# Scatter of the edge counts of a graph network: pieces of 127 sorted keys in place of 128

## The reference

```python
h = relu(layernorm(x))                                   # before each of the four
x = x + L0(h):  m = h[src] + edge_attr_96
                aggr = segment_sum(m, dst, 6250);  relu(aggr @ W1 + b1) @ W2 + b2 + (1 + eps) * h
x = x + L1(h):  msg = relu(h[src] + edge_attr_32 @ We + be)
                aggr = segment_sum(msg, dst, 6250);  two products, batch norm, relu
x = x + L2(h):  three graph convolutions: segment_sum(dinv[row] * dinv[col] * hw[row], col, 6250)
x = x + L3(h):  three attention layers: softmax over the edges of each target, weighted sum of h[src]
```

## Time and profile before

| what | us |
|---|---|
| median of the 2 runs | 12576.79 |
| the 2 runs | 12553.91 and 12599.67 |
| span of the profiled execution, first to last instruction | 12571.5 |
| GpSimd busy in it | 7982.0 (63%) |
| TensorE busy | 6178.3 (49%) |
| VectorE busy | 5097.4 (41%) |
| ScalarE busy | 4054.9 (32%) |

### The profile page before, as it was taken

The page is one execution under the profiler, slowest core; times in us unless marked ns, Lnnn a source line. Parts: engine busy times, 40 slices in busy tenths (PEclk is TensorE's granted clock), DMA queues, the critical chain, the costliest instruction groups (busy, mean ns, idle before and its releaser), DMA issues.

```text
span 12571.5 us, 140237 instructions
## 1 busy us (share of the span) xinstructions
PE 6178.3 (49%) x36085; PEld 5371.9 (43%) x36085; DVE 5097.4 (41%) x15838; ACT 4054.9 (32%) x10426; POOL 7982.0 (63%) x8396
## 2 busy tenths in 40 slices
PE   0199731255555567999344444433444334443443
PEld 0188621234444445777333333333334333343333
DVE  8455400033222224222444444444444444444444
ACT  0199400034444440000333333333333323333332
POOL 1877777557777750000677777667777766777775
PEclk8555665666666667999555555555555555555555
DMA  8044421222222214666222222222222222222222
GB/s 278 17 103 104 126 83 39 56 44 53 53 53 53 53 38 131 210 209 217 63 68 68 67 68 68 56 66 68 67 68 68 67 54 67 68 68 68 67 68 59
DMA packets 1053014, 1038.73 MB, mean 83 GB/s; under 512 B 641834, under 2 KB 758358, under 8 KB 1052336
## 3 DMA queue, kind: packets, MB, share of 16 engines
q1 hardware_dynamic: 704544, 611.05, 16.6%
q0 software_dynamic: 264160, 337.47, 13.2%
q10 hardware_dynamic: 83664, 82.78, 2.0%
HBM read 935.74 MB, written 96.55 MB: 82 GB/s over the span
## 4 chain that ended last, share of the span: by engine, by line
POOL 60%; issue 21%; PE 11%; DVE 4%; ACTq 2%; DMA 1%; ACT 0%; DVEq 0%; POOLq 0%; SPq 0%; PEldq 0%
POOL sb_HG L565 47%; POOL edge_counts L626 13%; PE sums L975 3%; ACTq L651 2%; PE psA L975 1%; PE psB L975 1%; PE sums L912 1%; PE psD L975 1%; PE psC L975 1%; PE psA L860 1%; DVE sb_ACC L1942 0%; PE psD L894 0%; PE psD L870 0%; PE psC L870 0%; PE psB L886 0%
## 5 line engine op out<-in xcount | busy, mean ns | idle before, releaser
L565 POOL DMA_INDIRECT sb_HG<-attention_table,sb_NOW x4992 | 4731.8, 948 | 1574.4 <-issue 1516.5
L912 PE MATMUL sums<-sb_HG 128*128 128x100 f32 x9984 | 2068.6, 399 | 443.9 <-ACT sb_HG L695 426.6
L912 PEld LDWEIGHTS sums<-sb_HG 128*128 128x128 f32 x9984 | 2035.4, 313 | 453.9 <-ACT sb_HG L695 435.6
L626 POOL DMA_INDIRECT edge_counts<-sb_HG x1625 | 1632.3, 1005 | 764.8 <-issue 495.0
L691 ACT ACTIVATE sb_H<-sb_iota_row,sb_H 128x128 f32<-128x128 f32 x6656 | 2029.1, 388 | 137.7 <-PE sums L912 63.9
L565 POOL DMA_INDIRECT sb_HG<-feature_table,sb_NOW x1612 | 1522.0, 944 | 556.3 <-issue 490.8
L1942 DVE TENSOR_TENSOR sb_ACC<-sb_ACC,sums 128x100 f32 x4992 | 1274.1, 255 | 1152.5 <-PE sums L912 619.0
L922 PEld LDWEIGHTS sums<-sb_HG 128*128 128x128 f32 x6656 | 1324.8, 299 | 315.4 <-issue 315.4
L922 PE MATMUL sums<-sb_HG 128*128 x6656 | 1340.6, 384 | 144.0 <-ACT sb_HG L695 71.3
L760 ACT ACTIVATE psC<-sb_SB 128x128 f32<-128x128 f32 x156 | 43.8, 281 | 3935.1 <-DVE sb_SB L1895 3935.1
L1487 DVE TENSOR_TENSOR sb_ACC<-sb_ACC,sums 128x97 f32 (+1 forms) x3328 | 848.0, 255 | 605.1 <-PE sums L922 135.9
(11 more groups left out here) (442 smaller groups left out, 9019.0 us busy)
## 6 DMA issues: line engine op xcount, KB each, us to landing
sb_HG<-edge_counts SPq DMA_DIRECT2D x1152, 256.0 KB, 3.3
sb_H<-rel_rows SPq DMA_DIRECT2D x312, 512.0 KB
sb_HG<-attention_table,sb_NOW POOLq DMA_INDIRECT x4992
sb_HG<-in_edge_attr_dram SPq DMA_DIRECT2D x201, 384.0 KB, 3.5
edge_counts<-sb_LW ACTq DMA_DIRECT2D x12, 6272.0 KB, 42.5
edge_counts<-sb_HG POOLq DMA_INDIRECT x1625
sb_HG<-feature_table,sb_NOW POOLq DMA_INDIRECT x1612, 2.5
sb_EA<-in_edge_attr_dram SPq DMA_DIRECT2D x201, 128.0 KB, 2.5
```

What stands on the lines that cost most here:

```text
L565: pool.indirect_dma_start(to, None, rows, bass.IndirectOffsetOnAxis(ap=index, axis=0)).then_inc(landed, 16)
L626: pool.indirect_dma_start(every_count, bass.IndirectOffsetOnAxis(ap=slot_of[:, f:f + 1], axis=0), tally[:, f:f + 1], None).then_inc(scatte ...
L912: last = nc.tensor.matmul(bank[:, k // 4, k % 4 * width:(k % 4 + 1) * width], HOT[:, hot, k, :], G[:, slot, k, 0:width], start=True, stop= ...
```

## The change

```diff
     CHUNKS = SORTED // P
+    CHUNK = P - 1
+    assert CHUNK * CHUNKS >= EF
...
-                    for f in range(p, SORTED, P):
-                        pool.indirect_dma_start(every_count, bass.IndirectOffsetOnAxis(ap=slot_of[:, f:f + 1], axis=0),
-                                                tally[:, f:f + 1], None).then_inc(scattered[n % 2], 16)
+                    for c in range(CHUNKS):
+                        f = P * c + p
+                        pool.indirect_dma_start(every_count, bass.IndirectOffsetOnAxis(ap=slot_of[0:CHUNK, f:f + 1], axis=0),
+                                                tally[0:CHUNK, f:f + 1], None).then_inc(scattered[n % 2], 16)
...
-                part, to = slice(c * P, (c + 1) * P), slice(c % 4 * P, (c % 4 + 1) * P)
-                nc.tensor.transpose(sums[c // 8][:, c // 4 % 2, to], low[:, part], ident[:, :])
-                nc.tensor.transpose((psA, psB, psC, psD)[c // 4][:, to], place[:, part], ident[:, :])
+                part, to = slice(c * CHUNK, (c + 1) * CHUNK), slice(c % 4 * P, (c % 4 + 1) * P)
+                nc.tensor.transpose(sums[c // 8][0:CHUNK, c // 4 % 2, to], low[:, part], ident[:, :])
+                nc.tensor.transpose((psA, psB, psC, psD)[c // 4][0:CHUNK, to], place[:, part], ident[:, :])
...
-                v.tensor_copy(last_of_run[:, part], sums[c // 1024][:, c // 512 % 2, 0:n])
-                last = v.tensor_copy(low_[:, part], (psA, psB, psC, psD)[c // 512][:, 0:n])
+                v.tensor_copy(last_of_run[0:CHUNK, part], sums[c // 1024][0:CHUNK, c // 512 % 2, 0:n])
+                last = v.tensor_copy(low_[0:CHUNK, part], (psA, psB, psC, psD)[c // 512][0:CHUNK, 0:n])
```

More of the change, by code:

```diff
@@ L1283, in _ @@
                 part = slice(c, c + n)
-                v.tensor_copy(last_of_run[:, part], sums[c // 1024][:, c // 512 % 2, 0:n])
-                last = v.tensor_copy(low_[:, part], (psA, psB, psC, psD)[c // 512][:, 0:n])
+                v.tensor_copy(last_of_run[0:CHUNK, part], sums[c // 1024][0:CHUNK, c // 512 % 2, 0:n])
+                last = v.tensor_copy(low_[0:CHUNK, part], (psA, psB, psC, psD)[c // 512][0:CHUNK, 0:n])
             link(last)
[L1287 to L1290, removed]
+            link(v.tensor_scalar(place_[0:CHUNK, :], last_of_run[0:CHUNK, :], (1 << TALLY_BITS) - 1, None, ALU.bitwise_and))
+            link(v.tensor_copy(tally[0:CHUNK, :], place_[0:CHUNK, :]))
+            link(v.tensor_scalar(place_[0:CHUNK, :], last_of_run[0:CHUNK, :], TALLY_BITS, LO_BITS, right, left))
+            v.tensor_tensor(slot_of[0:CHUNK, :], place_[0:CHUNK, :], low_[0:CHUNK, :], both).then_inc(slots_ready, 1)
             dve.wait_ge(slots_ready, 1)
```

## The result

The changed kernel takes 15,942 us at the median of 2 runs (15,931 to 15,952) against 12,577 us, a ratio of 1.266 with a 95% interval of 1.264 to 1.268. It is slower by 27%, where 12,090 us were forecast, and lies outside the range.

A forecast was written before the change was run, and what follows sets the result against it. GpSimd's scatter of 1625 indirect DMAs was taken as the bound; 0.30 us saved on each, 488 us, took the span from 12571.5 to 12083.5, and 5.3 more for the median gave 12,090 us, range 11,900 to 13,200.

The forecast's parts named there:

- The bound: GpSimd's scatter, 1625 DMAs: its end sets the start of everything behind it, so savings per scatter arrive one for one.
- Transposes and copies at nothing: Transposes and VectorE's copies before the scatter: costed at nothing, hidden by 68 us of zero filling; 0.1 us without that.
- Thirteen pads less, 12 us at most: Scatter: fewer indices per DMA save at most 7.5 ns each, 12 us over 1625.
- 127 can't be shared evenly, so one engine may get all: Scatter DMA: 127 is prime, so shares become uneven (fifteen of 8, one of 7) or one engine gets all 127.
- 18 packets per scatter: Scatter DMA of 127 indices: 2 or so packets of data on one engine and 16 of completion, where 128 made 32.
- two thirds, 0.30 us, to go with the fifteen shares that are no longer written: GpSimd's time per scatter: 0.30 of 0.45 us saved, instruction 0.66 us, 488 us over 1625 scatters.
- The split of 0.51 us fixed and 0.45 us for the form: GpSimd's 959 ns per scatter: 0.51 us taken as independent of the form, 0.45 us left for shares and entries.
- the slower one: Rival for the scatter, chance 0.30: one engine's entries are written one after the other, 119 more steps; 13,157 us at least.
- lowest price, 3 ns a step: Slower rival's scatter: 119 steps at 3 ns add 0.36 us each, 580 us in all, giving 13,157 us.
- its own next figure, 10 ns: Slower rival's scatter: at 10 ns a step, 1.19 us more per scatter, giving 14,511 us.
- waits for `scattered`: Sign that the forecast is wrong: waits for this completion semaphore (L618) appearing between the batches of scatters.
- The engines as a bound: Scatter transfer on one DMA engine: 0.38 us of engine time, under the 1.26 us between two, so not the bound.

The follow-up runs named there:

- E1: Kernel before the change, with only the scatter cut to indices 0 to 126: 15,924 us, ratio 1.2665.
- E2: Changed kernel with all its edits, but 126 indices per scatter: 12,608 us, ratio 1.003.
- E5: Kernel before the change, with only the scatter cut to 64 indices: 12,466 us in one run.
- E3: Kernel before the change, with only the scatter cut to 122 indices: 13,964 us in one run.
- E4: Kernel before the change, with only the scatter cut to 125 indices: 12,978 us in one run.
- E7: Changed kernel with four completion semaphores in place of two, changed after every five scatters inside a batch: 15,144 us, ratio 1.2046.

## Why the prediction was wrong

- *The bound, right.* The end of the scatter sets all that follows: the last scatter moved by 3341 us, L1's first gather by 3346.
- *Transposes and copies at nothing, right.* E1 has none of these edits and the same time; E2 has all of them and is within 0.3% of the kernel before.
- *Thirteen pads less, 12 us at most, unimportant.* With 16 engines halving the indices moved a scatter by 62 ns (E5), about 1 ns per index.
- *127 can't be shared evenly, so one engine may get all, right in its first half.* One engine gets the real entries (E1, E3, E4 in bytes and steps). From the rule of the Trainium skill on the number of engines ("DMA: Bandwidth & Descriptors", section "Why a DMA increments its semaphore by 16 and not by 1") I had 18 packets per scatter. The traces agree with the rule for k at 16, 14, 5, 2 and 1, but the packets are 48: by the bytes, the engines that take no part get as many empty entries.
- *The step that failed: "two thirds, 0.30 us, to go with the fifteen shares that are no longer written".* The fifteen shares are still written, each as long as the one that counts. Nothing is saved and 119 steps are added: 1.59 us at the median scatter, and 2561 us more of busy time over all 1625, where 488 us less had been forecast. The split of 0.51 us fixed and 0.45 us for the form, taken from a GpSimd copy, was wrong too: at 8 steps the form costs about 0.1 us (8 x 13.4 ns), and 0.85 us is fixed.
- *The rival that came true was the slower one.* Its condition (eight steps serve 16 engines now, one engine needs 127) fits all that was measured. Its lowest price, 3 ns a step, was the time an entry takes on an engine, and GpSimd's price is 13.4. At that price it gives 1625 x 1.59 = 2584 us and 15,161 us, within 17 us of E7, which has the steps and no pauses. It had a chance of 0.30. I put the range's end at the lowest price, where its own next figure, 10 ns, would already have lain above it.
- *Missing altogether: the pauses.* They are 783 us, idle time that the sum had no term for. I had named waits for `scattered` as a way to be wrong, but these are none: the landing waits never held GpSimd. No row of before could show a pause, as no batch had more than 585 entries for an engine.
- *The engines as a bound, right to be left out but with a wrong figure.* I had 0.38 us of engine time for all of a scatter; it is 1.36 us on each of the 16 engines, still under the 2.85 us between two.

## What to carry to other kernels

Give an indirect DMA on GpSimd a number n of indices that 16 divides, or at least one whose n/k is small, where k is the largest number up to 16 that divides n. GpSimd's time for one is about 0.85 us and 13.3 ns for each of n/k steps, so a scatter of 126 costs 3% more than one of 128, one of 122 costs 74% more and one of 127, a prime, 166% more; a gather, tried at 127 alone, costs 169% more. Padding to 128 is nearly free, and leaving indices out saves nearly nothing: 64 cost 6% less. Where many such DMAs complete on one semaphore, count n/k + 1 entries for each and expect a pause of 2.4 to 5 us whenever the sum would reach 1024. Shorter stretches per semaphore avoided it here; that this is safe under a larger load was not tried.

## What the runs showed of the hardware that was not expected

- By the bytes, engines that take no part in an indirect DMA get as many entries as those that do, 4 bytes each: 12.38 MB more in the changed kernel, 7618 bytes per scatter. The same sum comes out at 126, 125, 122 and 113 indices, and on gathers.
- GpSimd pauses when the entries for one engine would reach a limit between 1018 and 1024, counted only within a stretch on one semaphore: every 7 scatters at 128 entries per engine, 8 at 114, 16 at 62, 39 at 26, 113 at 9. A change of the semaphore starts the count anew without any wait (E4 between batches 0 and 1, E7).
- The duration of an indirect DMA hardly depends on the indices it carries as long as 16 engines share them: 897 ns for 64, 959 ns for 128.
